# A decoder layer pipelined over samples: the second local attention half a period behind the first

## The reference, cut to what matters

```
def self_attn(x, weight):                 # 16 heads, q = k = the slice of x, v = all of x
    y = heads(x)                          # (16, 128, 8)
    attn = softmax(y @ y.T / sqrt(8))
    return concat(attn @ x) @ weight      # 16*128 -> 128
def cross_attn(q, ctx):                   # 16 heads of 8, band |i-j| <= 64, then Wo and bo
def layer(x, ...):                        # twice
    q, k, v = split(shift_token(x) @ wqkv)          # 8 heads of 64
    q, k = rope(l2norm(q) * qs), rope(l2norm(k) * ks)
    x = x + local_attention(q, k, v) @ wo           # keys i-64 .. i
    h = layernorm(shift_token(x)) * lg + lb
    a, g = split(h @ w1 + b1)
    return x + (a * gelu(g)) @ w2 + b2
x = layernorm(x + self_attn(x)); x = layernorm(x + cross_attn(x, ctx))
x = layernorm(x + layer(layer(x)))
```

## Time and profile before

| | us |
|---|---|
| median of 3 runs | 1466.55 (1461.12 to 1466.93) |
| the profiled execution | 1461.15 |
| its span | 1459.3 |
| busy: PE, DVE, ACT, POOL | 1333.5, 1026.3, 938.5, 885.3 |

### The profile page before, as it was taken

The page is one execution under the profiler, slowest core; times in us unless marked ns, Lnnn a source line. Parts: engine busy times, 40 slices in busy tenths (PEclk is TensorE's granted clock), DMA queues, the critical chain, the costliest instruction groups (busy, mean ns, idle before and its releaser), DMA issues. The chain is left out here.

```text
span 1459.3 us, 39524 instructions
## 1 busy us (share of the span) xinstructions
PE 1333.5 (91%) x12472; PEld 928.8 (64%) x12472; DVE 1026.3 (70%) x2900; ACT 938.5 (64%) x2563; POOL 885.3 (61%) x1291
## 2 busy tenths in 40 slices
PE   5889999999999999999999999999999999998864
PEld 3556666666666666666666666666666666666543
DVE  2467776777777777777777777777777777776431
ACT  1256765677776667777766677776666777765552
POOL 2046666666666666666667666666666666666542
PEclk8799999999999999999999999999999999998785
DMA  5000000000000000000000000000000000000000
GB/s 158 10 5 4 5 7 7 5 4 5 4 4 5 5 5 5 4 4 4 5 5 5 5 5 4 4 4 5 5 5 5 4 5 3 5 5 3 3 3 4
DMA packets 22220, 12.55 MB, mean 9 GB/s; under 512 B 5878, under 2 KB 21024, under 8 KB 22176
## 3 DMA queue, kind: packets, MB, share of 16 engines
q1 hardware_dynamic: 21600, 10.96, 2.6%
q10 hardware_dynamic: 576, 1.05, 0.2%
HBM read 9.91 MB, written 2.10 MB: 8 GB/s over the span
## 5 line engine op out<-in xcount | busy, mean ns | idle before, releaser
L1212 POOL TENSOR_TENSOR local_e<-local_e,local_rd 128x512 f32<-128x512 f32 x128 | 133.0, 1039 | 238.2 <-DVE local_rd L1033 238.2
L848 ACT ACTIVATE local_e<-local_ps,local_bias,local_rn 128x128 f32<-128x128 f32 x512 | 230.8, 482 | 7.3 <-DVE local_bias L1029 7.3
L1191 POOL TENSOR_TENSOR local_rn<-local_sc,half_neg 128x8 f32<-128x8 f32 x128 | 211.3, 1658 | 14.4
L586 PE MATMUL self_ps<-self_z,self_e 128*128 128x129 f32 x1024 | 155.8, 291 | 2.6 <-ACT self_e L779 1.4
L1024 DVE TENSOR_REDUCE local_m<-local_ps 128x4 f32<-128x512 f32 x128 | 87.8, 686 | 96.4 <-PE local_ps L509 96.4
L586 PEld LDWEIGHTS self_ps<-self_z,self_e 128*128 128x128 f32 x1024 | 130.7, 196 | 13.8 <-issue 2.7
L955 DVE SCALAR_TENSOR_TENSOR self_y<-self_ps,self_rd,self_y 128x128 f32<-128x128 f32 x448 | 133.3, 345 | 8.8 <-issue 0.6
L606 PE MATMUL local_ps<-wz,self_kT 128*128 128x512 f32 x256 | 134.1, 627 | 1.1 <-ACT local_v L832 0.6
L848 ACT ACTIVATION_READ_ACCUMULATOR local_e<-local_ps,local_bias,local_rn 128x1 f32 x512 | 117.4, 229 | 0.0
L828 ACT ACTIVATE local_sq<-local_ps 128x512 f32<-128x512 f32 x128 | 76.1, 595 | 61.4 <-PE local_ps L665 58.4
L665 PE MATMUL local_ps<-wqkv_s,local_xT 128*128 128x512 f32 x128 | 71.4, 639 | 26.6 <-ACT local_xT L824 26.6
(11 more groups left out here) (172 smaller groups left out, 3392.6 us busy)
## 6 DMA issues: line engine op xcount, KB each, us to landing
self_xin<-x SPq DMA_DIRECT2D x32, 64.0 KB, 1.8
cross_cin<-ctx_in SPq DMA_DIRECT2D x32, 64.0 KB, 1.8
out<-local_out SPq DMA_DIRECT2D x32, 64.0 KB, 1.6
wqkv_s<-wqkv SPq DMA_DIRECT2D x2, 768.0 KB
wz<-w_heads ACTq DMA_DIRECT2D x4, 256.0 KB, 6.3
w_r<-w SPq DMA_DIRECT2D x2, 341.0 KB
con<-consts SPq DMA_DIRECT2D x1, 640.0 KB, 6.0
wo_s<-wo SPq DMA_DIRECT2D x2, 256.0 KB
```

The costliest lines, as they stand in the source:

```text
L586: last = nc.tensor.matmul(bank[:, 129 * j:129 * j + 129], s.e[:, h0 + j, :], s.z[:, h0 + j, :], start=True, stop=True)
L848: nc.scalar.activation(s.e[:, a, p, :], bank[:, 128 * p:128 * p + 128], ACT.Exp, bias=s.bias[:, a, p:p + 1], scale=s.rq[:, a, p:p + 1], ac ...
L1191: nc.gpsimd.tensor_tensor(s.rn[:, heads], s.sc[:, heads], half_neg[:, 0:LH], ALU.pow).then_inc(done, 8)
L1212: nc.gpsimd.tensor_tensor(s.e[:, a, :, :], s.e[:, a, :, :], s.rd[:, a, :].unsqueeze(2).to_broadcast([128, LH // 2, 128]), ALU.mult)\
```

## The change

Pieces and skews are cut anew. S becomes four: X (load copy, transpose, and GpSimd's low-precision copies), Z (the values), S (scores and exponentials) and U (the products with the values, the sum over heads, the norm). X, Z and S stay one iteration behind the load, U goes to the second, beside C. D becomes D (scores and exponentials) and G (the rest), E becomes E and F; F goes from the fourth to the fifth iteration. The number of iterations stays at 37. `LAST` stays 5.

The MLPs change banks: the first layer's now works in cross's banks, the second's in self's. The waits follow (`lent` with an own lag for each, `LENT`).

The addition of eps moves from GpSimd to VectorE, behind each `bn_aggr` (five a period), and so does the maximum with 1e-24, behind each sum of squares (four a period).

All four order strings are new. The diff, cut to its core (the same names are used below):

```
-MLP_LAG = 2 * STEP
-LETTERS = ("ADMO", "BENP")
-SKEW = {"S": 1, "C": 2, "A": 3, "D": 3, "M": 3, "O": 4, "B": 4, "E": 4, "N": 5, "P": 5}
+LETTERS = ("ADGMO", "BEFNP")
+SKEW = {"X": 1, "Z": 1, "S": 1, "U": 2, "C": 2, "A": 3, "D": 3, "G": 3, "M": 3, "O": 4, "B": 4, "E": 4, "F": 5, "N": 5, "P": 5}
+LENT = (STEP * (SKEW["M"] - SKEW["C"]), STEP * (SKEW["N"] - SKEW["X"]))
-    "OONAAONASPBPABPBCZSCBZSZZASACSBBDCSECSSCSDSDSDCSDEEMCCECME")
+    "UAUOUFUFUOUFAOFXANBACBCZZNBPCAABCDZCPZCPBBSCESGCSGCGSCGMSM")
...
-            s.m0, s.m1 = (SELF, CROSS)[l].b0, (SELF, CROSS)[l].b1
+            s.m0, s.m1 = (CROSS, SELF)[l].b0, (CROSS, SELF)[l].b1
...
+            def self_scores(v):
+                if behind(v, LENT[1] - STEP):
+                    pe.wait_ge(LOC[1].resid, v - (LENT[1] - STEP))
+                yield from core16(SELF, v)
...
                 if l == 0:
-                    pe.wait_ge(SELF.acc, lent(v))
+                    pe.wait_ge(CROSS.resid, lent(v, LENT[0]))
                 else:
-                    pe.wait_ge(CROSS.resid, lent(v))
+                    pe.wait_ge(SELF.acc, lent(v, LENT[1] - STEP))
+                    pe.wait_ge(SELF.xT_ready, lent(v, LENT[1]))
...
-                nc.vector.bn_aggr(s.mv[:, :], s.st[:, 0, :]).then_inc(s.moments, 8)
+                nc.vector.bn_aggr(s.mv[:, :], s.st[:, 0, :]).then_inc(s.moments, 4)
+                dve.wait_ge(s.moments, v + 12)
+                nc.vector.tensor_scalar(s.ve[:, :], s.mv[:, 1:2], EPS, None, ALU.add).then_inc(s.moments, 4)
...
-                        .then_inc(s.square_sum, 8)
+                        .then_inc(s.square_sum, 4)
+                    dve.wait_ge(s.square_sum, v + 8 * a + 4)
+                    nc.vector.tensor_scalar(s.sc[:, LH * a:LH * a + LH], s.ss[:, LH * a:LH * a + LH], 1e-24, None, ALU.max)\
+                        .then_inc(s.square_sum, 4)
...
                 pool.wait_ge(moments_done, v + STEP)
-                nc.gpsimd.tensor_scalar(s.ve[:, :], mv[:, 1:2], EPS, 1.0, ALU.add, ALU.mult).then_inc(done, 8)
-                yield
-                pool.wait_ge(done, v + 8)
-                nc.gpsimd.tensor_tensor(out, s.ve[:, :], half_neg[:, 0:1], ALU.pow).then_inc(done, 8)
+                nc.gpsimd.tensor_tensor(out, ve[:, :], half_neg[:, 0:1], ALU.pow).then_inc(done, STEP)
```

More of the change, by code:

```diff
@@ L417, in decoder_kernel, with stages @@
         N_PREP_P = 5
-        def stages(eng, order, prepare_local, self_stage, cross_stage, attention_head, attention_tail, mlp_head, mlp_tail, self_values=None):
+        def stages(eng, order, prepare_local, self_head, self_values, self_scores, self_tail, cross_stage,
+                   attention_head, attention_scores, attention_tail, mlp_head, mlp_tail):
             def iteration(i):
                 parts = {}
-                if at(i, SKEW["S"]) is not None:
-                    parts["S"] = self_stage(at(i, SKEW["S"]))
-                    if self_values is not None:
-                        parts["Z"] = self_values(at(i, SKEW["S"]))
-                if at(i, SKEW["C"]) is not None:
-                    parts["C"] = cross_stage(at(i, SKEW["C"]))
+                for letter, part in zip("XZSUC", (self_head, self_values, self_scores, self_tail, cross_stage)):
+                    v = at(i, SKEW[letter])
+                    if v is not None and part is not None:
+                        parts[letter] = part(v)
                 for l in range(2):
-                    for letter, part in zip(LETTERS[l], (attention_head, attention_tail, mlp_head, mlp_tail)):
+                    for letter, part in zip(LETTERS[l], (attention_head, attention_scores, attention_tail, mlp_head, mlp_tail)):
                         v = at(i, SKEW[letter])
-                        if v is not None:
+                        if v is not None and part is not None:
                             parts[letter] = part(l, v)
@@ L1143, in self_stage, with self_tail @@
                 yield
-                yield from inverse_root(s, v, s.moments, s.mv, s.rs[:, :], s.rstd)
+            def self_tail(v):
+                s = SELF
+                inverse_root(s, v, s.moments, s.ve, s.rs[:, :], s.rstd)
                 yield
@@ L1224, in mlp_head @@
                 yield
[L1225 removed]
+                inverse_root(s, v, s.mid_moments, s.ve2, s.rs2[:, :], s.mid_rstd)
                 yield
```

74 lines of the change are left out of this document (42 added, 32 removed).

## The result

| | before | after |
|---|---|---|
| median, us | 1463.84 (1460.59 to 1466.93) | 1538.76 (1536.97 to 1539.25) |
| span of the profiled execution | 1459.3 | 1537.1 |
| mean granted clock of TensorE | 0.965 | 0.936 |

The ratio is 1.051, 95% interval [1.0488, 1.0531]. The change costs 75 us; I had forecast 1465, no change, and a range of 1442 to 1492.

What follows compares the result with a forecast made beforehand. TensorE was taken as the bound: 39.2 us of work plus 2.0 end wait plus 0.9 smaller waits, period 42.1; +2.7 over 27 periods, ends -1, from 1461.15 to 1463, +2 for the median: 1465 us, range 1442 to 1492.

Steps and rivals of the forecast that it cites:

- The blocks and the chains at the end of the iteration: TensorE has 39.2 us of work a period; ScalarE's and the norm's chains end 2.0 us behind its full queue.
- The three starts: After the first layer's V product: shift at 4.2 us, second turned scores at 4.6, transpose behind the norm at 6.9 to 7.1.
- the 1.1 us ahead of the K products: Old wait between the first layer's transpose and its K product, for ScalarE's copy; forecast to go, 1.0 us a period.
- the second values step: Self's second values step, end of the iteration: forecast 8.05 us after the first layer's V product starts, not 6.04.
- The sum of the ends: Time outside the 27 loop periods, at start and end together: forecast to change by -1 us, with 6 to either side.
- the nine small operations: Eps additions and floors moved from GpSimd to VectorE: 0.25 us each, 2.2 a period, no bound, path gain under 0.1.
- The walk: Step-by-step timing from the first layer's V product to self's second values step; puts 2.0 us of waiting in each period.
- the first values step "at 7.2": Self's first values step, directly behind the transpose after the norm: forecast 7.2 us after the first layer's V product starts.
- GpSimd's run: 16 back-to-back instructions, 15.8 us, against about 15.3 of TensorE work; as rival, it becomes the bound: 1485 to 1497, chance 0.16.
- The banks: Rival: second MLP returns self's banks late for self's scores; 0.5 us a period, 1475 to 1480; 0.12 with other lost tenths.
- The slower side: All slower outcomes, chance 0.30: GpSimd 0.16, banks and other lost tenths 0.12, the load of exp 0.02.
- The smaller waits: Four steps where TensorE waits for a releaser, plus longer handoffs: 0.9 us a period, between 0.2 and 2.0.

Runs made afterwards that it cites:

- run 13: Changed kernel with the floor as a reduction, the first layer's transpose moved behind the loop's end, three empty products (unread identity matmuls) ahead of it: 1463.86 us, ratio 1.0001.
- run 8: Kernel before, old order, with only the five additions of eps moved to VectorE and the floor left on GpSimd: 1483.36 us, ratio 1.0163.

## Why the prediction was wrong

- **The blocks and the chains at the end of the iteration: right.** The three starts agree to 0.1 us, the wait stood where I put it, and the 1.1 us ahead of the K products are gone. With the three causes out the second values step comes at 8.08 in run 13 (I said 8.05), the period is 42.26 (I said 42.1) and the time 1463.4 to 1463.9 (I said 1465). The sum of the ends is right partly by luck: it differs by 0.6 us (I said -1 +- 6), but the stretch behind the last self transpose is 5.9 us shorter (165.0 for 170.9) and what lies ahead of the 27 periods 6.5 longer.
- **The term that was mis-sized: the nine small operations.** I took 0.25 each between 0 and 0.33, called VectorE "no bound" and put them at a gain under 0.1 on the path. The five additions take 0.15. The four floors take 0.66 in the mean, up to 1.02, twice and three times my upper bound. I took the 0.25 from the earlier trace rows, a reciprocal that reads PSUM, and the upper bound from the earlier trace rows, the price on GpSimd: neither has VectorE work SBUF to SBUF while GpSimd works. What the floor paid was the rest of GpSimd's instruction, for which 1.04 to 1.66 us stood in the earlier trace rows. It is worth 20 to 29 us.
- **The step that was missing: the clock.** The walk put 2.0 us of waiting at the end of the iteration and priced it at its length. The sum kept the upper level of the clock, which the earlier trace rows had shown for the old order, for the matmuls behind it. A fall costs 1.5 us, and keeping the clock up is worth 37 to 46 us in all. This is the largest of the three. What sets this wait apart from those of the old order stays open, for there two waits of 0.62 and 0.81 us with one transpose between them left TensorE no busier in 3 us than the new wait does (1.62), and the clock stayed up in all twenty periods:

```profile
653.80:656.80 3.00, 1.57 (x8) 0.97 (x8) 2.33 (x9) 1.12 (x5) 2.00 (x7) 1.00 0.00 0
```

- **The step that was passed over: the first values step "at 7.2".** The order shows the loop's branch between transpose and values step, and I gave it no price: in the old order, behind eight matmuls, it cost 0.1 us. Behind one transpose it is 0.34 to 0.37 us a period, 9 to 10 us.
- **The rivals.** GpSimd's run didn't decide: against the smallest distance of that step, self's first scores lose 0.1 us a period. The first run shows how near it was: with the nine operations back on GpSimd, the wait for its scaling ahead of self's first scores grows by 23 us and the time by 55. The banks cost nothing that I could find. The slower side was right in sign and had 0.30; none of its mechanisms was the one.
- **The smaller waits: about right.** The period of run 13 leaves 42.26 - 39.2 - 2.0 = 1.1 us for them (I said 0.9). Against the smallest distance of each step, cross's denominators lose 0.45 there (I said 0.2 to 0.4), the others outside the walk 0.12 or less each.

## What to carry to other kernels

Price an operation that is moved between VectorE and GpSimd by what the other engine is running, not by its own size, and look for a form that isn't held: a reduction over pairs in place of an elementwise maximum was worth 20 to 29 us with the same result. Where a change makes a new wait on TensorE, ask what the clock does behind it, and compare the granted clock of stretches of some 3 us, not the mean of the span, which moved from 0.965 to 0.936 only. And see what TensorE still has to do at the loop's end: behind eight matmuls it cost 0.1 us, in a wait nothing that could be seen, behind a single transpose 0.4.

## What the runs showed of the hardware

- TensorE's granted clock fell to its lower level behind a wait of 1.06 us in a loop that was otherwise nearly full: in 20 of 20 periods, in 17 or 18 with the hold gone, in 4 or 6 with two empty products in the wait (0.43 us left empty), in none with three or four. In the old order, with waits of 0.62 and 0.81 us close together, it fell in none. One fall cost 1.0 to 1.6 us.
- An elementwise maximum of 128x8 from SBUF to SBUF on VectorE took 170 ns beside an idle GpSimd; beside a working one it ended 0.02 to 0.03 us after GpSimd's running instruction and took up to 1018 ns. A product of two 128x4 tiles did likewise, up to 898 ns. A 128x1 addition (153 to 155 ns) and a reduction of 128x16 (169 to 172 ns) did not.
- An addition on VectorE that waits for the 0.15 us aggregate ahead of it started 0.25 us after it (run 8), where an independent product started 0.08 after it (before).
- The end of the hardware loop on TensorE cost 0.37 us behind a single transpose (0.57 to the next start instead of 0.20) and 0.1 behind eight matmuls.
